# One of seven query blocks summed by the vector engine, along the slots of the exponentials

## What is computed

```
def _L3_conv_ref(x, q_w, k_w, v_w):
    xf = x.reshape(b, din, hw)
    Q = jnp.einsum('kc,bcp->bkp', q_w, xf)
    K = jnp.einsum('kc,bcp->bkp', k_w, xf)
    V = jnp.einsum('vc,bcp->bvp', v_w, xf)
    S = jnp.einsum('bkp,bkq->bpq', Q, K)
    A = jax.nn.softmax(S, axis=-1)
    z = jnp.einsum('bpq,bvq->bvp', A, V)

x = x + _L3_conv_ref(_gn(x), L3_conv_q_w, L3_conv_k_w, L3_conv_v_w)
```

## Time and profile before

| | |
|---|---|
| median of 3 runs | 1879.36 us (1878.1 to 1879.47) |
| the profiled execution | 1879.96 us, with a span of 1878.2 us |
| TensorE busy (matmuls) | 1646.5 us, 88% of the span |
| VectorE busy | 1258.0 us, 67% |
| ScalarE busy | 1249.8 us, 67% |
| GpSimd busy | 1099.3 us, 59% |
| mean granted TensorE clock | 0.95 of full |

### The profile page before, as it was taken

How to read it: one execution, slowest core, us unless ns; L and a number is a source line. 1 busy time by engine, 2 the same in 40 slices (tenths; PEclk the granted TensorE clock), 3 DMA queues, 4 the chain that set the end, 5 groups by cost and what they waited for, 6 DMA issues and landing times.

```text
span 1878.2 us, 35981 instructions
## 1 busy us (share of the span) xinstructions
PE 1646.5 (88%) x10840; PEld 826.0 (44%) x10840; DVE 1258.0 (67%) x2446; ACT 1249.8 (67%) x2324; POOL 1099.3 (59%) x898
## 2 busy tenths in 40 slices
PE   5887899999887699999988779999999787999997
PEld 4363344444436344444444534444454353444442
DVE  5947777775584777777467477777748657777760
ACT  2036788888412788888831278888872347888885
POOL 3610577778651067777855006777777402677777
PEclk9988899999889899999998889999999898999998
DMA  2004000000000400000000040000000011000000
GB/s 84 0 1 86 2 7 6 6 6 7 11 0 1 86 1 6 6 6 7 11 7 1 1 85 1 6 6 11 6 6 6 0 27 26 6 6 6 6 6 11
DMA packets 10104, 26.91 MB, mean 14 GB/s; under 512 B 2256, under 2 KB 6608, under 8 KB 9424
## 3 DMA queue, kind: packets, MB, share of 16 engines
q1 hardware_dynamic: 9936, 24.79, 5.5%
HBM read 8.73 MB, written 6.42 MB: 8 GB/s over the span
## 4 chain that ended last, share of the span: by engine, by line
PE 54%; issue 15%; DVE 12%; POOL 9%; ACT 9%; POOLq 1%; DVEq 0%; ACTq 0%
PE PS L1239 22%; PE PS L1163 11%; PE PS L1195 10%; DVE nmt L672 4%; ACT PS L854 3%; DVE nmt L665 2%; ACT Pb L897 2%; PE PS L1060 2%; POOL VT L970 2%; POOL VT L965 2%; PE PS L1135 2%; POOL VT L967 2%; POOL VT L974 1%; POOL accP L1008 1%; PE PS L1126 1%
## 5 line engine op out<-in xcount | busy, mean ns | idle before, releaser
L665 DVE TENSOR_REDUCE nmt<-PS 128x1 f32<-128x448 f32 x1176 | 680.3, 620 | 280.8 <-PE PS L1163 276.4
L1008 POOL TENSOR_TENSOR accP<-accP,Pb 128x512 f32<-128x512 f32 (+1 forms) x532 | 678.3, 1275 | 168.1 <-ACT Pb L897 144.6
L897 ACT ACTIVATE Pb<-PS 128x896 f32<-128x896 f32 (+1 forms) x700 | 638.9, 914 | 130.2 <-PE PS L1195 107.9
L1239 PE MATMUL PS<-Pb,VT 128*64 128x448 f32 x2800 | 656.0, 548 | 4.4 <-ACT Pb L897 3.6
L1163 PE MATMUL PS<-Ka,Qa 96*64 96x448 bf16 x2744 | 480.9, 362 | 55.9 <-DVE nmt L665 28.1
L1195 PE MATMUL PS<-Qa,Ka 99*64 99x448 bf16 x2744 | 489.8, 358 | 5.3 <-ACT Qa L869 4.0
L854 ACT ACTIVATE PS<-PS,nmt 128x448 f32<-128x448 f32 x588 | 356.3, 606 | 56.8 <-DVE nmt L672 29.4
L1163 PEld LDWEIGHTS PS<-Ka,Qa 96*64 96x64 bf16 x2744 | 159.4, 111 | 324.3 <-issue 127.2
L1195 PEld LDWEIGHTS PS<-Qa,Ka 99*64 99x64 bf16 x2744 | 162.3, 111 | 248.8 <-issue 184.3
L1239 PEld LDWEIGHTS PS<-Pb,VT 128*64 128x64 f32 x2800 | 191.6, 138 | 96.2 <-ACT Pb L897 24.5
L777 ACT ACTIVATE xnp<-xw,nb,rstd 128x448 f32<-128x448 f32 x56 | 40.5, 750 | 204.9 <-DVE nb L487 204.9
(11 more groups left out here) (141 smaller groups left out, 1435.0 us busy)
## 6 DMA issues: line engine op xcount, KB each, us to landing
xin<-in_x SPq DMA_DIRECT2D x4, 1568.0 KB, 12.2
out<-xw SPq DMA_DIRECT2D x28, 224.0 KB, 1.9
Qa<-parts SPq DMA_DIRECT2D x24, 168.0 KB, 6.9
Ka<-parts SPq DMA_DIRECT2D x24, 112.0 KB, 3.8
Ka<-parts SPq DMA_DIRECT2D x24, 84.0 KB, 2.6
wz<-in_weights SPq DMA_DIRECT2D x1, 829.0 KB, 8.2
Qa<-parts SPq DMA_DIRECT2D x24, 28.0 KB, 1.9
cs<-in_cst SPq DMA_DIRECT2D x1, 576.0 KB, 8.8
```

The source lines that it names most:

```text
L665: nc.vector.reduce_max(nmt[:, target % 2, b, t:t + 1], PS[0:BLK, bank, 0:CH], X, negate=True).then_inc(mx_free, 1)
L897: nc.scalar.activation(Pb[0:r, j % PSLOTS, :, :], PS[0:r, 2 * (k % 2):2 * (k % 2) + 2, 0:CH], ACT.Exp).then_inc(exp_done, 1)
L1008: nc.gpsimd.tensor_tensor((accQ if j < TO_ACCP else accP)[0:r, :, REST:CH], (accQ if j <= TO_ACCP else accP)[0:r, :, REST:CH], Pb[0:r, j % ...
L1239: last = mm(PS[C * h:C * h + C, OB, 0:CH], VT[:, j, C * h:C * h + C], Pb[:, j % PSLOTS, h, :], start=(j == 0), stop=(j == NQ - 1))
```

## The change

The scalar engine sums two query blocks instead of three. Block 2 (columns DVE_COL = 128 to REST = 192) is now summed by the vector engine, out of `Pb`: after steps 2, 7, 12, ... one sum over slots 0 to 2, after steps 4, 9, 14, ... one over slots 3 and 4, each into its own one of ten places of a new tensor `pd`, and after the last step one sum over the ten places into `accP`. In a sum over slots the neighbours that are added lie one slot apart. After the last key block, of 64 keys, the two halves of the partitions are summed apart. GpSimd keeps its four blocks, and now also multiplies the tile sums with their factors. The exponential that writes a slot again waits for the vector engine too, on a new semaphore `psum_dve`. GpSimd's loop over the middle superblocks is written out. TensorE's ones product has 320 columns instead of 256.

```diff
-ACT_BLOCKS = 3
+ACT_BLOCKS = 2
 ACT_TILES = ACT_BLOCKS * NJ
-REST = ACT_BLOCKS * C
+DVE_COL = ACT_BLOCKS * C
+REST = DVE_COL + C
+EARLY_SLOTS = 3
...
+def dve_sums_upto(j):
+
+    if j >= NQ - PSLOTS + EARLY_SLOTS:
+        return DVE_GROUPS + 1
+    return 2 * (j // PSLOTS) + (1 if j % PSLOTS < EARLY_SLOTS else 2)
+
+
+DVE_GROUPS = 2 * NQ // PSLOTS
+DVE_SUMS = DVE_GROUPS + 2
...
+        pd = sb("pd", [QC, DVE_GROUPS, 2, C])
...
+            dve.sem_inc(psum_dve, DVE_SUMS)
...
-                def column_sums(sidx, s):
-
-                    dve.wait_ge(ef_ready, sidx + 1)
-                    nc.vector.tensor_tensor(sme[:, :, :], sm[:, s % 2, :, :], ef[:, :, :], ALU.mult).then_inc(dstep, 1)
+                def sum_slots(sidx, j):
+
+                    dve.wait_ge(exp_done, NQ * sidx + j + 1)
+                    i = dve_sums_upto(j) - 1
+                    if i == 0:
+                        dve.wait_ge(psum_dve, DVE_SUMS * (sidx + 1))
+                    if j == NQ - 1:
+                        i, r = DVE_GROUPS - 1, key_rows(j)
+                        nc.vector.reduce_sum(pd[0:r, i, :, :], Pb[0:r, EARLY_SLOTS:PSLOTS, :, DVE_COL:REST]
+                                             .rearrange("p s h c -> p h c s"), X).then_inc(psum_dve, 1)
+                        nc.vector.reduce_sum(pd[r:QC, i, :, :], Pb[r:QC, EARLY_SLOTS:EARLY_SLOTS + 1, :, DVE_COL:REST]
+                                             .rearrange("p s h c -> p h c s"), X).then_inc(psum_dve, 1)
+                    else:
+                        first, end = (0, EARLY_SLOTS) if j % PSLOTS < EARLY_SLOTS else (EARLY_SLOTS, PSLOTS)
+                        nc.vector.reduce_sum(pd[:, i, :, :], Pb[:, first:end, :, DVE_COL:REST]
+                                             .rearrange("p s h c -> p h c s"), X).then_inc(psum_dve, 1)
+
+                def sum_groups(sidx):
+
+                    dve.wait_ge(psum_dve, DVE_SUMS * (sidx + 1) + DVE_GROUPS + 1)
+                    dve.wait_ge(d_ready, sidx + 1)
+                    nc.vector.reduce_sum(accP[:, :, DVE_COL:REST], pd[:, :, :, :].rearrange("p i h c -> p h c i"),
+                                         X).then_inc(psum_dve, 1)
+
+                def column_sums(sidx):
+
                     dve.wait_ge(dstep, sidx + 1)
                     nc.vector.reduce_sum(dcol[:, :], sme[:, :, :], X).then_inc(dcol_ready, 1)
...
                         if s == NJ - 1 and more:
                             front_at(j)
+                        if j == 0 and s:
+                            sum_groups(sidx - 1)
+                        if j % PSLOTS in (EARLY_SLOTS - 1, PSLOTS - 1):
+                            sum_slots(sidx, j)
                         for target, i, n_reduced, _, bank, _ in TILES_AT.get(NQ * s + j, ()):
                             max_tile(target, i, n_reduced, bank)
...
+                sum_groups(NJ * g + NJ - 1)
                 reciprocals(NJ * g + NJ - 1, 7)
...
                         act.wait_ge(psum_pool, POOL_SUMS * (sidx + (j >= PSLOTS)) + pool_sums_upto((j - PSLOTS) % NQ))
+                        act.wait_ge(psum_dve, DVE_SUMS * (sidx + (j >= PSLOTS)) + dve_sums_upto((j - PSLOTS) % NQ))
...
+                def scale_sums(sidx, s, first):
+
+                    pool.wait_ge(ef_ready, sidx + 1)
+                    if not first:
+                        pool.wait_ge(dcol_ready, sidx)
+                    nc.gpsimd.tensor_tensor(sme[:, :, :], sm[:, s % 2, :, :], ef[:, :, :], ALU.mult).then_inc(dstep, 1)
+
                 def superblock(sidx, s, first, front=False):
                     for j in range(1, NQ):
+                        if j == SUM_STEP:
+                            scale_sums(sidx, s, first)
...
-                with pool.Fori(1, NJ - 1) as s:
+                for s in range(1, NJ - 1):
                     superblock(NJ * g + s, s, False)
...
                     pe.wait_ge(psum_pool, POOL_SUMS * (sidx + 2))
+                    pe.wait_ge(psum_dve, DVE_SUMS * (sidx + 2))
                     for h in range(2):
-                        last = mm(PS[C * h:C * h + C, bank, REST:CH], ones[:, :], accP[:, h, REST:CH], start=True, stop=True)
+                        last = mm(PS[C * h:C * h + C, bank, DVE_COL:CH], ones[:, :], accP[:, h, DVE_COL:CH],
+                                  start=True, stop=True)
```

More of the change, by code:

```diff
@@ L345, in build @@
         psum_pool = sem("exps_summed_by_pool")
+        psum_dve = sem("exps_summed_by_vector")
         first_summed = sem("first_max_scores_summed")
@@ L744, in superblock @@
                         if j == SUM_STEP:
-                            column_sums(sidx, s)
+                            column_sums(sidx)
                 for i in range(TILES):
```

## The result

| | before | after |
|---|---|---|
| median (4 runs each, on the same chip) | 1879.41 us (1878.1 to 1880.94) | 1912.03 us (1909.87 to 1912.5) |
| ratio, 95% interval | | 1.0173 (1.0156 to 1.0189) |
| span of the profiled execution | 1878.2 us | 1910.3 us |
| VectorE busy | 1258.0 us, 67% | 1426.6 us, 75% |
| ScalarE busy | 1249.8 us, 67% | 1119.4 us, 59% |

The account below looks back on a forecast made before the run. TensorE bounds a middle superblock (floor 39.3 of 42.6 us), standing only some 3.3 us. Superblock 0 -8, middle +4, front +10, ends +1, last +0.6 make +8: 1887 us, range 1848 to 1970.

Parts of the forecast that it names:

- the border term of +0.9: Steps 24 and 0: two sums (0.70) and the sum of ten (1.48) before tiles cost TensorE +0.9 us per middle superblock.
- rival C: Much slower: every element read with a distance costs twice 1.04 ns, deciding from 1.5 ns; 1961 us, chance 0.35.
- The scalar engine's relief: Middle superblock: fewer tile sums give TensorE 0.96 us, 0.6 at step 23 and 0.36 at step 15.
- 0.42 + 0.3: Middle superblock: 0.42 us for a slot sum at steps 3 to 5, +0.3 for step 19's before the maxima splitting.
- The front: Last superblock of the first three groups, with the next group's front work: 3.4 us each, together +10.
- (a): Front: next input's statistics wait behind step 24's sum, delaying the sum of ten and TensorE's denominators: +0.9 us per group.
- (b): Front: step 17's sum awaits an exponential behind root and table load, delaying filter parts and TensorE's transposition: about 2.5 us lost.
- the 0.65: Front: TensorE transposes the spatial filter's parts 0.65 us behind their end in the kernel before.
- Superblock 0: First superblock of each of four groups: scalar engine's relief gives 2 us of waits of 5.2, together -8.
- Group ends: At a group's end the sum of ten is ready 0.3 us later than GpSimd's last addition: +1 in all.
- Rival B: Faster: scalar engine's 1.3 us per middle superblock go whole, new sums fit idle time; 1853 us, chance 0.20.
- Rival D: Exponentials wait for unsummed slots, only near the front's step 19, about 1 us in three groups: 1890 us, no separate chance.

Follow-up runs that it names:

- pd_innermost: Changed kernel with the ten partial sums of an output side by side, 4 bytes apart, against the change as made: 1890.01 us, ratio 1.0059 to the kernel before.
- no_sum_of_ten: front_order with the sum of ten partial sums left out and the slot sums kept (third block's denominators not computed): 1854.24 us, ratio 0.9866.
- running_after: front_order with the sum of ten split into four running sums and a last sum of two, all sums behind their step's tiles: 1857.8 us, ratio 0.988.
- front_order: Changed kernel with the next input's statistics at step 23 of the superblock before and the root behind step 17's exponential: 1893.95 us, ratio 1.0079.
- root_late: Changed kernel with only the scalar engine's root moved behind the exponential of step 17: 1904.53 us, ratio 1.0134.

## Why the prediction was right and wrong

The forecast was +8 and the result +32.6, so 24.6 us are missed: 8.7 in the 20 superblocks 1 to 5, 10.8 in the front superblocks, 2.2 in superblock 0, 3.3 at the groups' ends, and -0.4 at the program's. The step that failed is the price of the sum of ten: "No extra cost is seen, [...] I take 1.04" ns an element, against 1.75 measured, and with it the border term of +0.9. pd_innermost, in which that sum takes the forecast's 1.48 us, runs in 1890 us, next to the forecast's 1887. That it comes so near is in part luck: its middle superblocks are 0.55 us shorter than forecast (42.35 for 42.9), its front ones 1.3 longer, and superblock 0 gives back less.

- **The sign and the sum of work: right.** The new work was put at +6.0 us of the vector engine per superblock and came to +5.8. Slot sums at 0.55 and 0.42 us measured 0.586 and 0.416. The step "no extra cost is seen, I take 1.04" held for 11 of the 12 instructions.
- **The sum of ten: mis-sized.** 1.48 us forecast, 2.39 measured, since its ten places cost 1.67 to 1.75 ns an element. pd_innermost shows that layout alone makes the difference. The prediction had such a price as rival C, but for every sum, hence its 1961: C was right about a price of 1.5 ns or more and wrong about which sums it meets. The choice of 1.04 from a row with neighbours side by side was right for two and three places by luck as much as by reason: the one row with a distance could not tell, as the prediction says.
- **The border term: mis-sized.** +0.9 forecast for the sum of ten and the sums of step 24 together; +1.8 measured for the sum of ten (no_sum_of_ten) and 0.2 for those of step 24. 0.85 of it goes with the extra 0.91 us of the sum (pd_innermost); the rest, about 1.1, is near the forecast's own term. The reasoning on the border was sound and its input was not.
- **The relief and the slot sums: near.** The scalar engine's relief was put at 0.96 and came to 1.15, the multiplication at 0.60 and 0.7. The slot sums away from the border were put at 0.42 + 0.3, and all eleven cost 0.55, of which 0.3 lie near step 5 and none at steps 19 to 21: in the steady steps they hide, as said, and before the splitting of the maxima too, which was not. The middle superblock misses by 0.3 (42.9 forecast, 43.2 measured): 0.9 from the sum of ten, less 0.3 of relief, less 0.17 of slot sums, less 0.13 by which the forecast was too high, since -0.60 + 0.42 is -0.18 and not its -0.05. With superblock 5, where the growth is 1.0 and no row of its own was read, the 20 superblocks give +12.7 for +4.
- **The front: right places, wrong size.** Together +10 forecast, +20.8 measured; per group 3.4 and 7.0. (a) The superblock begins 1.2 us later than in the kernel before (453.7 for 452.5). With that, "the statistics end near 456.3" is right (457.2), and "the sum of ten at 457.7" failed: it takes 2.3 us and ends at 459.8, and the stand is 1.91 for 0.9. (b) "2.5 is lost" became a stand of 3.48. The filter parts did start late by what was said: 490.46 - 487.69 = 2.8 us behind the root's end. By the prediction's own terms this less 0.65 is 2.1, and its 2.5 is not derived. What failed is the 0.65 taken as TensorE's arrival behind the parts: the earlier trace rows show it in a stretch in which the kernel before had lost 1.7 us of pace (0.50 of full from 485.40 to 488.80). After, the same stretch runs at full clock, TensorE arrives earlier, and the gain in pace is spent in the stand. Besides, the pace lost behind a stand stood in no term of the sum: there is one low stretch more than before, 1.7 us. 1.0 at (a), 1.0 at (b) and 1.7 of pace are 3.7 of the 3.6 missed per group.
- **Superblock 0: nearly right.** -2 forecast, -1.45 on average measured.
- **Group ends: too low.** +1 forecast. +4.3 measured. At 508.43 TensorE waits 1.26 us for the sum of ten where 0.3 was forecast, and three groups make 3.8 of it. The sum is 0.9 longer than priced, here too. But the stretch between groups varies by a few us from kernel to kernel, so that the rest of the 4.3 fits so well says little.
- **Rival B** (faster) failed on its own condition: the tiles of step 0 are late by a sum of 2.4 us, where it allowed 0.7. running_after, where that sum is 0.42 us and stands behind the tiles, comes within 5 us of its 1853, with the front's order changed as well. **Rival D**, an exponential waiting for the vector engine because of a slot, is there and small: 2.4 us in five places of the whole program, three in superblock 0 and two in the program's last superblock, and none at the front's step 19, where it was expected.
- **Tests named ahead.** "TensorE's waits for L854 fall to less than half" is wrong (2.6 to 2.8), since late maxima come back as late sums; "those for the maxima rise by 1 to 1.5" is too low (3.0 to 5.0). The first transposition comes 10.8 us after the root's end where it came 8.8 before: 1.9 later, for the 2.5 named.

## What to carry to other kernels

Price a moved piece of work by its place in an in-order queue, not by its amount: here 5.7 us in eleven pieces cost 0.55 us, and 2.4 us in one piece, in front of tiles that another engine awaits, cost 1.8. Split it, put it behind what others wait for, and look at what stands next in the queue as well. When a sum reads along a slow axis, count the places it visits before it returns; in these float32 sums three were free, four were not. And where the trace shows stretches at the lower clock, as here, give them a term of their own when a change adds a stand of TensorE.

## What the hardware showed that was not expected

- The vector engine's float32 sums take 1.02 to 1.12 ns an element from two or three interleaved places and 1.66 to 1.75 ns from four to ten. Three and five places cost the same at 512 and 3584 bytes apart, ten at 512 and 1792. A single sum of 512 elements takes 0.68 us at 4 and 8 bytes and 1.04 at 16. Writing 40 bytes apart cost nothing over 128 partitions (587 and 418 ns); only the one sum that copies 128 elements, on 64 partitions, went from 283 to 379.
- After stands of 1.91 and 3.48 us TensorE's granted clock was 0.50 of full for 3.4 us, and after one of 0.85 us in the kernel before as well. After stands of 1.85 us in front_order, 1.86 in root_late and 1.16 in pd_innermost it was 1.00. So the length of the stand alone does not decide it, and what does was not tested.
- A row of the waits can name the engine that is relieved while the cause sits on another. The same row read 2.8 us with the sums and 1.8 without, the scalar engine's work being the same.
